# Gated cross-attention layer on one core: the twelve products with A of a pair are issued between the first twelve FFN products of a step

## The reference

```python
Q, K, V = einsum('bshd,hde->bshe', layernorm(x) | ctx | ctx, Wh)      # 4 heads of 128
scores  = einsum('bshe,bthe->bhst', Q, K) / sqrt(128)
A = maximum(abs((scores * decay[None]).sum(axis=0)), 1.0)             # one A for all 64 sequences
O = einsum('hst,bthe->bshe', A, V).reshape(b, s, 512)
Y = (O - mean(O)) / sqrt(var(O) + 1e-3) * gamma + beta
x = x + tanh(g_xattn) * ((relu(layernorm(x) @ wg) * Y) @ wo)
g = (layernorm(x) @ gate_w.T) * gate_s;  u = (layernorm(x) @ up_w.T) * up_s        # 1408 wide
x = x + tanh(g_ffn) * ((silu(g) * u) @ down_w.T * down_s)
```

## Time and profile before

| what | value |
|---|---|
| median of three runs | 1441.88 us |
| the profiled execution, its span | 1447.4 us |
| TensorE busy | 1420.4 us, 98% |
| VectorE busy | 1043.3 us, 72% |
| ScalarE busy | 726.3 us, 50% |
| GpSimd busy | 735.3 us, 51% |
| mean granted TensorE clock | 0.998 of full |

### The profile page before, as it was taken

The page is one execution under the profiler, slowest core; times in us unless marked ns, Lnnn a source line. Parts: engine busy times, 40 slices in busy tenths (PEclk is TensorE's granted clock), DMA queues, the critical chain, the costliest instruction groups (busy, mean ns, idle before and its releaser), DMA issues.

```text
span 1447.4 us, 20320 instructions
## 1 busy us (share of the span) xinstructions
PE 1420.4 (98%) x7097; PEld 728.3 (50%) x7135; DVE 1043.3 (72%) x1562; ACT 726.3 (50%) x1145; POOL 735.3 (51%) x734
## 2 busy tenths in 40 slices
PE   8999999999999999999999999999999999999998
PEld 4666666665445544455444444444444444444443
DVE  7788998878477676766776677564867768768762
ACT  5566565554555635455463545534344444443442
POOL 5656769863564445444553554434137237137235
PEclk9999999999999999999999999999999999999999
DMA  8999898973878796987888897886383473572432
GB/s 275 344 336 306 292 317 318 343 251 130 276 204 263 227 276 206 260 276 210 248 274 237 264 243 222 247 252 164 112 228 115 124 224 122 139 218 98 139 109 89
DMA packets 372920, 324.96 MB, mean 225 GB/s; under 512 B 259280, under 2 KB 285264, under 8 KB 372816
## 3 DMA queue, kind: packets, MB, share of 16 engines
q1 hardware_dynamic: 355248, 291.63, 66.2%
q10 hardware_dynamic: 17568, 31.99, 6.2%
HBM read 209.14 MB, written 114.43 MB: 224 GB/s over the span
## 4 chain that ended last, share of the span: by engine, by line
PE 74%; DVE 10%; DMA 6%; SPq 3%; issue 3%; ACT 2%; POOL 2%; ACTq 0%; DVEq 0%; POOLq 0%
PE ps L2067 24%; PE po L2067 8%; PE pyb L1930 7%; PE ps L2074 7%; PE ptb L2074 5%; PE pyb L2074 5%; PE ps L1988 5%; PE po L1930 3%; PE pyb L2058 3%; PE ptb L2058 3%; DMA wy_scratch<-misc 2%; SPq L510 2%; DVE reg L1129 1%; PE ptb L2062 1%; PE pyb L2062 1%
## 5 line engine op out<-in xcount | busy, mean ns | idle before, releaser
L2067 PE MATMUL ps<-x2t,gate 128*128 128x512 f16 x704 | 166.6, 379 | 1.2 <-DVE tmp L1436 1.1
L1930 PE MATMUL pyb<-xnt,wgs 128*128 128x512 f16 x708 | 166.3, 380 | 1.4 <-DVE wgs L1153 1.3
L2067 PE MATMUL ps<-op,wbuf 128*128 128x512 f16 x704 | 166.3, 379 | 0.5 <-issue 0.5
L2067 PE MATMUL ps<-x2t,up 128*128 128x512 f16 x704 | 166.3, 379 | 0.0
L1800 POOL TENSOR_TENSOR p5b<-p5b,p1b 128x512 f32<-128x512 f32 x44 | 55.7, 1265 | 209.1 <-ACT p5b L860 209.1
L1816 POOL TENSOR_TENSOR hid<-tmp,hid 128x512 f16<-128x512 f32 x88 | 104.6, 1190 | 105.9 <-ACT hid L836 105.9
L2074 PE MATMUL ps<-down_first,hid 128*128 128x512 bf16 x683 | 152.4, 379 | 2.1 <-POOL hid L1816 0.8
L1811 POOL TENSOR_TENSOR hsp<-hall,hsp 128x640 f16<-128x640 f32 (+2 forms) x72 | 123.6, 1731 | 37.1 <-ACT hsp L887 37.1
L2067 PE MATMUL po<-op,wbuf 128*128 128x512 f16 x528 | 129.0, 379 | 0.6 <-DVE u2b L1383 0.6
L1436 DVE SCALAR_TENSOR_TENSOR tmp<-ps,colsb,tmp 128x512 f32<-128x512 f32 x88 | 65.4, 744 | 68.2 <-PE ps L2067 62.3
L1988 PE MATMUL ps<-reg 128*128 128x256 f32 x768 | 109.7, 294 | 4.3 <-DVE reg L1129 3.8
(11 more groups left out here) (218 smaller groups left out, 2764.2 us busy)
## 6 DMA issues: line engine op xcount, KB each, us to landing
wbuf<-ws_scratch SPq DMA_DIRECT2D x44, 896.0 KB, 5.0
xr<-in_x SPq DMA_DIRECT2D x62, 512.0 KB, 6.3
raw<-in_ctx_t SPq DMA_DIRECT2D x32, 512.0 KB, 5.6
v_scratch<-tmp ACTq DMA_DIRECT2D x64, 256.0 KB, 6.0
raw<-v_scratch SPq DMA_DIRECT2D x32, 512.0 KB, 6.6
x_scratch<-xr SPq DMA_DIRECT2D x32, 512.0 KB, 4.8
xr<-x_scratch SPq DMA_DIRECT2D x32, 512.0 KB, 5.9
raw<-w_scratch SPq DMA_DIRECT2D x31, 512.0 KB, 6.0
```

Source lines behind the costliest of these rows:

```text
L1930: last = e.matmul(dst, lhs[a], rhs[b], start=(k == 0 and i == 0), stop=(k == n - 1 and i == 2))
L2067: last = e.matmul(dst, upper(wt), act[i], start=start, stop=stop and exact, skip_group_check=True)
```

## The change

`o(q)` is taken apart into its waits (`o_ready`) and its twelve products (`o_term`). In the first groups, for q > 3, a step with piece 0 passes q to `up_mm` or `down_mm` as `beside`. These take the waits of `o_ready` first, then their own, and issue one product with A behind each of their first twelve products. The order among the twelve is as before, and so are the products, their operands and their sums. The increments of `gm`, `um` and `dn` go to the same products as before. `o(q)` itself stays for q = 0 to 3.

```diff
--- before.py
+++ after.py
@@ -2009,15 +2009,24 @@
                 if 3 in ks:
                     last.then_inc(s["w"])
 
-            def o(q):
+            def o_ready(q):
                 p.wait_ge("vlo", q + 1)
                 p.wait_ge("alo", 1)
                 if q:
                     p.wait_ge("nr", 2 * q)
-                for h in range(4):
-                    last = three(po[:, h // 2, :, 128 * (h % 2):128 * (h % 2) + 128], [a[:, h, :] for a in a_parts],
-                                 [b[:, :, 128 * h:128 * h + 128] for b in vs_of(q)], 0, 1)
-                last.then_inc(s["o"])
+
+            def o_term(q, n):
+
+                h, (a, b) = n // 3, ((0, 0), (0, 1), (1, 0))[n % 3]
+                last = e.matmul(po[:, h // 2, :, 128 * (h % 2):128 * (h % 2) + 128], a_parts[a][:, h, :],
+                                vs_of(q)[b][:, :, 128 * h:128 * h + 128], start=(n % 3 == 0), stop=(n % 3 == 2))
+                if n == 11:
+                    last.then_inc(s["o"])
+
+            def o(q):
+                o_ready(q)
+                for n in range(12):
+                    o_term(q, n)
 
             def y_t(t):
                 p.wait_ge("nr", t + 1)
@@ -2083,8 +2092,11 @@
                 for _ in range(n):
                     e.matmul(banks[1], zero[:, 0:128], zero[:, 0:512], start=True, stop=True)
 
-            def up_mm(exact, g, j):
-                n = 15 * g + j
+            def up_mm(exact, g, j, beside=None):
+
+                n, m = 15 * g + j, 0
+                if beside:
+                    o_ready(beside)
                 if j == 0:
                     p.wait_ge("tb2e", 2 * g + 4)
                     if g == 0:
@@ -2105,11 +2117,17 @@
                     for k in range(4):
                         last = with_part(exact, banks[2 * (n % 2) + which], wt[:, k, 128 * j:128 * j + 128],
                                          [x2t[0][:, k, :], x2t[1][:, k, :]], i, i == 0 and k == 0, i == 1 and k == 3)
-                    if i:
-                        last.then_inc(s[("gm", "um")[which]])
-
-            def down_mm(exact, g, t):
+                        if i and k == 3:
+                            last.then_inc(s[("gm", "um")[which]])
+                        if beside and m < 12:
+                            o_term(beside, m)
+                        m += 1
+
+            def down_mm(exact, g, t, beside=None):
+
                 n = 15 * g + 11 + t
+                if beside:
+                    o_ready(beside)
                 sl = slice(128 * t, 128 * t + 128)
                 slot_free(p, n - 2)
                 p.wait_ge("hlo", 11 * g + 10)
@@ -2126,8 +2144,11 @@
                         for i in range(first, end):
                             last = down_part(exact, down_bank(4 * g + t), hid[part][i][:, sl], i, down_first[:, i, :],
                                              done == 0, done == 2 * NI - 1)
+                            if beside and done < 12:
+                                o_term(beside, done)
                             done += 1
-                last.then_inc(s["dn"])
+                            if done == 2 * NI:
+                                last.then_inc(s["dn"])
 
             def half_sums(exact, w, *sums):
 
@@ -2211,15 +2232,16 @@
             def first_groups(exact):
                 for g in range(NS):
                     for step in range(15):
+                        beside = None
                         for q, piece in pieces(15 * g + step):
                             if piece == 0 and q > 3:
-                                o(q)
+                                beside = q
                             if piece == 9:
                                 wo_pair(q)
                         if step < 11:
-                            up_mm(exact, g, step)
+                            up_mm(exact, g, step, beside)
                         else:
-                            down_mm(exact, g, step - 11)
+                            down_mm(exact, g, step - 11, beside)
 
 
             keep_busy(10)
```

## The result

The changed kernel takes 1449.63 us, the median of five runs (1447.39 to 1451.54), against 1441.88 us (1441.21 to 1445.92) in the same comparison: a ratio of 1.0046, 95% interval 1.0029 to 1.0063. It is slower by 0.5%. A second comparison on another occasion gave 1448.35 us against 1443.11 us, 1.0033 (1.0020 to 1.0045).

A forecast was written before the change was run, and what follows sets the result against it. TensorE, busy 98% of the span, was taken to set the end. 25 x 0.141 us for interleaving plus 0.70 us for lost cover gave +4.2 us, 1441.9 to 1446.1 us; range 1438 to 1450.5 us.

The forecast's parts named there:

- the forecast by itself: Whole kernel: 1446.1 us as the likeliest time, 1444.5 to 1447.5 us without the rivals, chance 0.60.
- rival C: Later statistics or changed phase against transfers make one more half-clock wait like that at 772: 1450 us, chance 0.18.
- Part 1: Interleaving on TensorE: each product with A goes from 0.120 to 0.132 us, +0.141 us a block, +3.9 us over 28.
- the upper bound of the estimate: Interleaved products with A: at most 0.135 us each, +5.0 us over 28 blocks.
- the sum: Pairs 7 to 31 at 25 x 0.141 us plus 0.70 us at pair 6: +4.2 us.
- Part 2: Waits the block covered: pair 4's returns but nothing is left by 408.25; pair 6 costs +0.70 us.
- two waits of rows 9: TensorE waits before output projections at 390.13 (0.86 us) and 408.25 (1.12 us), claimed to absorb the delay of pairs 4 and 5.
- all other steps pass their waits at once: Waits for the step's PSUM slot, now ahead of the products: passed at once in all but two of 28 steps.
- Part 3: A's result comes later, after 4.2 us instead of 1.44; VectorE's statistics and hidden tile slip, but hidden: cost 0.
- The profiled execution's own 4.6 us: Wait of 2.8 us before 772.14 and eight half-clock products, together about 4.6 us, which a faster execution may not have.
- Rival A: Both weight loads hidden at every interleaved product, 0.108 us each: price -4.1 us, 1438 us; chance 0.12.
- Rival B: Interleaved products cost only their entry price, 0.118 to 0.120 us each, plus 0.6 us at pair 6: 1442.5 us; chance 0.10.

The follow-up runs named there:

- half_between: The changed kernel with A and V as two f16 parts instead of fp32, products still one by one; 1441.18 us against 1443.11 us for the kernel before, ratio 0.9986.
- half_ahead: The kernel before with A and V as two f16 parts instead of fp32, block ahead of the step; 1439.22 us against 1443.11 us, ratio 0.9977.

## Why the prediction was right or wrong

The direction was right and the time, 1449.6 us, lies in the range, near its upper end; the likeliest time, 1446.1 us, was 3.5 us too low. That the range held is in part luck: the forecast by itself went to 1447.5 us, and the room above was made for rival C, which did not happen. By steps:

- **Part 1**, the mechanism, was right: every product with A became an exit, and entry and exit cost what rows 4 and 5 had shown. The size was short: 0.132 us a product was taken from exits out of a run, and a product that is entry and exit at once takes 0.135 us in up steps ((1.443 + 0.175) / 12), the upper bound of the estimate, and 0.133 in down steps. For pairs 8 to 31 the sum put 24 x 0.141 = 3.4 us, measured are 18 x 0.175 + 6 x 0.154 = 4.1 us.
- **Part 2** was right that pair 4's wait comes back in full, and wrong that nothing of it is left by 408.25. The sum let two waits of rows 9 take it up, and against the first profile they did (1.87 + 0.18 - 0.87 - 1.14 = 0.04 us). But the wait at 390.13 is in no other profile. Against the second and third profile of the kernel before, pairs 4 and 5 leave 1.97 + 0.18 - 0.75 = +1.4 us and 1.80 + 0.18 - 0.98 = +1.0 us. Nor is the wait at 408.25 a fixed store: 0.9 us of it stay in `half_between` in spite of the late pair 4, and in `half_ahead` it is gone without one. Pair 6 was put at +0.70 and came out at +0.54 and -0.05 us.
- What failed besides is the sentence that all other steps pass their waits at once. At pair 7, the first step of a group, up_mm waits for the transposed tile of L1324. Only the waits for the PSUM slot and for hlo had been held against the starts, not the wait for `tb2e`, whose row was there to be read. It would have given 0.67 us, though, and in two other profiles nothing; measured are +1.35 and +0.96 us, against 0.14 in the sum.
- **Part 3** was right. The statistics of pair 8 start 4.4 us after the step's first FFN product (466.64 against 462.24), the hidden tile behind them is late, and no step of TensorE from pair 8 on shows it.
- **The sum**: 4.2 us predicted, 5.3 to 6.5 measured in the steps, by the two profiles of the change and the second and third of the kernel before. The first profile of the change has +0.7 from the product's size, +1.2 from pair 7, -0.16 each at pair 6 and n = 86, and +1.4 or +1.0 from pairs 4 and 5; short waits that only one profile of before has take 0.9 or 0.3 us off. The 5.2 us between the second medians agree with it. The 7.7 us between the first ones are above it; in the profiles 0.9 to 1.3 us arise ahead of the stage, in code that both kernels share, and whether that holds for the medians isn't shown.
- **The profiled execution's own 4.6 us** at 772 us were rightly set aside: they are a chance of that execution. But the wait at 390.13, a chance of the same execution, was left in the sum. Whoever had compared the two first spans, 1447.4 and 1448.6 us, would have found the change nearly free.
- **Rival A** fell: no exit was free. The rule of the Trainium skill ("TensorE: Matmul & The Clock Gate", Back-to-back issue gap), 109 ns for a product of 256 columns, holds for the f16 products, 0.109 us each, but not for fp32 ones in either place. **Rival B** fell as well. **Rival C** did not happen: no wait like that at 772 is in either profile of the change.

Not settled is which property of an fp32 product holds up the following load, its weights or its moving operand: all experiments changed both together. The type fp32 by itself doesn't suffice: in rows 7 an f16 load goes under an fp32 transpose of 128 columns.

## What to carry to other kernels

Before interleaving two kinds of products, look in the trace for the places where they meet already, and price every new border by these; here hiding an fp32 load under a 16-bit product gained nothing: the product took 0.135 us instead of 0.120. Work that runs ahead of a wait is cover: for each place it is moved from, hold the release time of every wait of that step against its start, also those whose idle time in the profile is zero. Take a second profile of the kernel before, before a wait enters the sum: of the waits of the first one, that at 390 us was in no other, and that at 772 us had shrunk to 0.27 us in the second and was gone in the third. Where the price lies in a type, change the type: with f16 parts the block is 9% shorter wherever it stands.

## What the runs showed of the hardware

- An fp32 product of 256 columns takes 0.120 us in a run of its kind, 0.13 us as the last one ahead of a 16-bit product, and 0.133 to 0.135 us alone between two of them; the same product in f16 takes 0.109 us in all these places.
- The weight load of a 16-bit product begins 0.12 us after the start of an fp32 product with 256 columns, while the fp32 load (0.19 us) runs beneath a 16-bit product of 512 columns. An fp32 load that comes right behind a held-up 16-bit one has a record of 0.20 instead of 0.19 us.
- Steps bound by TensorE alone repeat from execution to execution: single steps with a pair within 0.009 us, their mean to 0.001 us. So a change of 0.06 us in a step is measured by one profile each, where twelve timed runs of the kernel leave an interval of 0.22 to 0.34% of 1443 us.
- Waits for work that hangs on loads from scratch memory don't repeat: the one at 772 us was 2.77, 0.27 and 0 us long in three profiles of one kernel, the one at 390 us 0.70, 0 and 0 us.
